# A graph network's node stages with two buffers instead of one, and its first table split inside the first gather pass

## The chip, the core and the metric

The kernel runs on one core of a Trainium2 chip. The metric is the device time of one execution in microseconds (us); here it is the median of three runs. Five engines work beside each other, each with its own queue: TensorE (PE) multiplies and transposes into PSUM, VectorE (DVE) and ScalarE (ACT) work element by element, GpSimd (POOL) does so too and issues the indirect DMAs, and SyncE (SP) issues most of the other DMAs. They meet only at semaphores.

## What is computed

Two layers of a graph network over 12500 nodes of 64 values and 412500 edges, sorted by their end node. The first is a hyperbolic attention layer, the second a message-passing layer with batch norms over edges and over nodes. Cut to what matters:

```python
h = jnp.maximum(_layernorm(x), 0.0)
# layer 0, over nodes
h = mobius_matvec(weight, h, C)                 # h @ weight.T, rescaled by row
# over edges: row = src, col = dst
dist = sqdist(h[edge[0]], h[edge[1]], C)
edge_e = jnp.exp(-leaky_relu(logmap0(C / (C + dist), C)[0], ALPHA))
h_prime = segment_sum(edge_e[:, None] * logmap0(h, C)[edge[1]], edge[0])
out = jax.nn.elu(h_prime / segment_sum(edge_e, edge[0])[:, None])
x = x + proj(expmap0(out, C), C)
h = jnp.maximum(_layernorm(x), 0.0)
# layer 1, over edges
e = _bn_relu(concat([h[src], h[dst], edge_attr]) @ Wm1 + bm1, gm1, betm1)
msg = _bn_relu(e @ Wm2 + bm2, gm2, betm2)
aggr = segment_sum(msg, src)
# over nodes; _bn_relu(x, gamma, beta) = relu(gamma * (x - mean) / sqrt(var + EPS) + beta)
u = _bn_relu(concat([h, aggr]) @ Wu1 + bu1, gu1, betu1)
x = x + _bn_relu(u @ Wu2 + bu2, gu2, betu2)
```

## The kernel before

The program is written engine by engine, in blocks (`nc.Block()`). Inside one, every engine runs its own list, and `end_phase` puts two barriers of all engines between stages. All order is written by hand: `wait_ge`, `hold` (a wait in a loop) and `consume` (a wait that takes its count back) are the waits, `chain` makes a queue wait for each of its own instructions.

Nodes stand as 98 chunks (NCH) of 128 partitions with D = 64 values each, and one chunk of padding (NC = 99). Node stages go over them in NIT = 7 rounds of CPI = 14 chunks, so one part is 128 x 896 numbers, or 128 x 1792 where rows are 128 wide. Edges stand in NBLK = 214 blocks of 16 tiles (TB) of 128 slots.

The stages in their order, with those that the change touches named in bold:

- **First node stage** (block at L249): layer norm, then seven rounds for the product with the weight. In each, VectorE copies the part to `stage` (L278), TensorE turns it by seven transposes into PSUM (L347), ScalarE copies that to `hT` (L326), TensorE multiplies (L351), VectorE copies the product out (L280). `stage`, `hT` and each PSUM area are single. Then row functions, and the table `h0_d` is stored.
- Sort of the edges into blocks (L462 on), 3000 us long.
- **First table** (block at L957), a stage of its own: SP loads the rows of `h0_d` into R0 (L960), and VectorE's `piece3` splits them into three bf16 numbers each, in T0 (L839 to L843, once for 6336 and once for 99 columns).
- **First gather pass** (block at L1045). GpSimd gathers the far node's row for each edge, 16 indirect DMAs a block (L1084), into four buffers G; TensorE picks the near node's row out of T0 with one-hots (L1126), in quarters of a block, into two PSUM areas; VectorE sums their three pieces (L1145) and multiplies with the gathered rows (L1151 to L1156). SP loads the records (L1049, L1064) and spreads slot numbers over the partitions for VectorE's one-hots (L1056, L1060, L1135). After three parts of the blocks and at the end VectorE computes distances (`part_weights`).
- Weights and first sums over edges (L1187 to L1363).
- **Middle stage** (block at L1372): division, elu, the second layer norm.
- **Second table** (block at L1428): the product of h with both halves of Wm1, seven rounds as in the first stage. VectorE copies one half out over a scratch tile into `b` (L1452, L1453), adds the bias to the other (L1454) and splits it by `piece3` into T1. When all is done SP stores `b` (L1438).
- Second gather pass, then two passes over edges with the batch norms of the messages.
- **Last stages** (blocks at L2037, L2090, L2117). The first adds the two halves of the sums (L2051), and in seven rounds VectorE puts h and the sums side by side in `stage` (L2054, L2056), TensorE turns (L2069), ScalarE copies (L2082), TensorE multiplies with Wu1 (L2074), ScalarE copies out with the bias (L2084). Then `node_stats` takes 25 lots of 500 nodes (L2026). The second does relu (L2094), product (L2106), copy out (L2096), and `node_stats` again. The third does relu (L2121), turns back (L2129), adds to X (L2138), and SP stores the whole result (L2145, L2146).

## Time and profile before

| what | value |
|---|---|
| median of 3 runs | 17072.78 us |
| lowest and highest | 17068.78 and 17084.48 us |
| the profiled execution's own time | 17093.01 us |
| its span in the trace | 17091.3 us |
| busy in the span: PE, DVE, ACT, POOL | 37%, 51%, 24%, 56% |

One execution was profiled; its rows carry every duration below, in us from the span's start. A row of the timeline has start, duration, engine and line, the tiles written and read, how many instructions were merged, and in brackets how long the engine stood idle before, and what released it. `SPq` is the issue of a DMA by SP; the DMA itself ends later, which shows in who waits for it. "remote" and "issue" are waits that the trace puts down to no instruction.

### The profile page before, as it was taken

How to read it: one execution, taken by the hardware profiler on the slowest of the kernel's cores; microseconds unless marked ns; L12 is line 12 of the kernel's file. 1: busy time of each engine (PE TensorE's matmuls, PEld its weight loads, DVE VectorE, ACT ScalarE, POOL GpSimd, SP SyncE). 2: the span in 40 equal slices, each digit the busy share in tenths (PEclk: the TensorE clock that was granted, in tenths of full speed). 3: DMA queues.
4: the chain of work that ended last, by engine and by line, in shares of the span. 5: the costliest groups of instructions: out<-in, count | busy, mean ns of one | idle time of the engine just before them, and what ended most of it. 6: DMA issues, size and time to landing. Idle time of an engine off the chain costs nothing. (4 is left out here: it accounts for less than half of the span.)

```text
span 17091.3 us, 195568 instructions
## 1 busy us (share of the span) xinstructions
PE 6354.3 (37%) x50077; PEld 5035.1 (29%) x50078; DVE 8652.0 (51%) x18303; ACT 4054.6 (24%) x7861; POOL 9635.6 (56%) x9968
## 2 busy tenths in 40 slices
PE   2444444311111111111159522323223223258996
PEld 2444444300000000000058511111111111125995
DVE  5888888623333333333268733333333333346884
ACT  1666666400000000000058400000000000024333
POOL 0555555466656665666657356666666666622773
PEclk7777777655555555555579756655655656579998
DMA  2000000133323332323444222222222222275331
GB/s 58 8 8 8 8 8 8 27 75 75 75 66 73 75 74 68 74 69 74 67 106 151 67 66 66 68 63 68 67 65 68 65 66 68 65 145 187 106 107 54
DMA packets 1142331, 1160.59 MB, mean 68 GB/s; under 512 B 688769, under 2 KB 832769, under 8 KB 1142018
## 3 DMA queue, kind: packets, MB, share of 16 engines
q1 hardware_dynamic: 845634, 680.39, 13.9%
q0 software_dynamic: 235008, 248.13, 8.6%
q10 hardware_dynamic: 61632, 231.44, 3.4%
q8 instruction: 20, 0.33, 0.0%
q14 instruction: 37, 0.30, 0.0%
HBM read 872.56 MB, written 286.75 MB: 68 GB/s over the span
## 5 line engine op out<-in xcount | busy, mean ns | idle before, releaser
L1559 POOL DMA_INDIRECT big<-b_d,big x3424 | 3284.0, 959 | 2270.7 <-POOLq L144 1232.2
L1084 POOL DMA_INDIRECT big<-h_d,big x3424 | 3273.9, 956 | 2001.9 <-issue 1189.0
L1145 DVE TENSOR_REDUCE ps<-ps 128x260 f32<-128x780 f32 x856 | 837.8, 979 | 3275.1 <-remote 1441.1
L1126 PE MATMUL ps<-big 128*128 x3424 | 737.9, 373 | 4609.0 <-issue 3388.5
L1686 DVE TENSOR_REDUCE ps<-ps 128x256 f32<-128x768 f32 x856 | 827.6, 967 | 2582.9 <-DVEq L144 1605.9
L1126 PEld LDWEIGHTS ps<-big 128*128 128x128 bf16 x3424 | 442.4, 162 | 4904.3 <-issue 4901.1
L1638 PE MATMUL ps<-big 128*128 x3424 | 608.7, 335 | 2615.9 <-issue 2130.1
L1885 POOL TENSOR_SCALAR big<-iota_f,big 128x128 f32<-128x128 f32 x1498 | 880.4, 608 | 827.7 <-DMA big<-rec_d 528.3
L1638 PEld LDWEIGHTS ps<-big 128*128 128x128 bf16 x3424 | 444.6, 160 | 2973.7 <-issue 2973.7
L777 ACT ACTIVATE big<-big 128x512 bf16<-128x512 bf16 x1736 | 1076.7, 708 | 907.1 <-ACTq L144 907.1
L1092 ACT ACTIVATE big<-big 128x16 int32<-128x16 f32 x214 | 49.1, 229 | 4899.9 <-issue 2304.5
L1620 PE MATMUL ps<-big 128*128 128x512 f32 x856 | 768.6, 1052 | 1134.6 <-PEq L144 1107.3
L1573 ACT ACTIVATE big<-ps 128x128 f32<-128x128 f32 x214 | 59.4, 278 | 4695.8 <-ACTq L144 4142.0
L747 PE MATMUL ps<-big 128*128 128x120 bf16 x12896 | 1001.4, 251 | 63.2 <-issue 59.3
L747 PEld LDWEIGHTS ps<-big 128*128 128x128 bf16 x12896 | 951.3, 118 | 87.9 <-issue 85.9
L825 POOL DMA_INDIRECT rec_d<-big x496 | 791.8, 1596 | 290.2 <-POOLq L144 160.6
L783 ACT ACTIVATE big<-big 128x512 bf16<-128x512 bf16 x1736 | 913.6, 614 | 0.0
L1283 POOL TENSOR_SCALAR big<-iota_f,big 128x128 f32<-128x128 f32 x856 | 691.1, 820 | 326.3 <-DMA big<-rec_d 288.5
L1358 PE MATMUL ps<-big 128*128 128x128 f32 x6848 | 815.8, 277 | 103.5 <-DVE big L1283 89.5
L810 POOL TENSOR_TENSOR big<-HA,big 128x624 bf16<-128x624 bf16 x124 | 153.3, 1236 | 1224.4 <-POOLq L144 1224.4
L1358 PEld LDWEIGHTS ps<-big 128*128 128x128 f32 x6848 | 782.8, 192 | 136.3 <-issue 134.0
L1961 PE MATMUL ps<-big 128*128 128x64 f32 x6848 | 789.1, 274 | 1.8 <-DVE big L1885 1.7
(409 smaller groups left out, 14488.7 us busy)
## 6 DMA issues: line engine op xcount, KB each, us to landing
big<-e_d SPq DMA_DIRECT2D x428, 512.0 KB, 3.1
rows_d<-big ACTq DMA_DIRECT2D x214, 544.0 KB
big<-rows_d SPq DMA_DIRECT2D x214, 544.0 KB, 3.2
HA<-slots_d SPq DMA_DIRECT2D x214, 512.0 KB
big<-slots_d SPq DMA_DIRECT2D x214, 512.0 KB
e_d<-big ACTq DMA_DIRECT2D x214, 512.0 KB
big<-rec_d SPq DMA_DIRECT2D x860, 64.0 KB, 2.9
big<-h_d,big POOLq DMA_INDIRECT x3424
```

The source lines that it names most:

```text
L747: m = t.matmul(o, DH[b][:, j * WS + w * P:j * WS + (w + 1) * P], EX[b][:, j * CH * L:(j + 1) * CH * L], start=False, stop=(j == J - 1))
L777: a.activation(DH[b][:, j * WS:(j + 1) * WS], iota_w, ACT.Square, scale=-1.0, bias=seg_f[b][:, j:j + 1]).then_inc(s_sq, 1)
L783: last = a.activation(o, o, ACT.Relu, scale=-1.0, bias=1.0)
L825: gp.indirect_dma_start(rec_d, bass.IndirectOffsetOnAxis(ix[b][:, w:w + 1], 0), stage[b][:, w * L * REC:(w + 1) * L * REC], None).then_inc ...
L1084: gp.indirect_dma_start(G[g][:, t * ROW:(t + 1) * ROW], None, h0_d, bass.IndirectOffsetOnAxis(idx[g % 2][:, t:t + 1], 0)).then_inc(gath[g] ...
L1126: m = t.matmul(XS[q % 2][:, n, 0:3 * D + 3], OT3[g % 2][:, o, :], T0[:, ds(chunks[o // 2] * TW, 3 * D + 3)], start=True, stop=True)
L1145: v.tensor_reduce(xrow[:, q * QT:(q + 1) * QT, :], XS[q % 2][:, :, 0:3 * D + 3].rearrange("p t (q w) -> p t w q", q=3), AX, ALU.add).then_ ...
L1358: m = t.matmul(ps[:, o:o + P], O4[g][:, n * P:(n + 1) * P], G0[g][:, n * ROW:n * ROW + P], start=(n % 2 == 0), stop=(n % 2 == 1))
L1559: gp.indirect_dma_start(G[g][:, t * D:(t + 1) * D], None, b_d, bass.IndirectOffsetOnAxis(idx[g % 2][:, t:t + 1], 0)).then_inc(gath[g], 16)
L1638: m = t.matmul(XST[q % 2][:, n // 2, n % 2, :], OT3[g % 2][:, o, :], T1[:, ds(chunks[o // 2] * (3 * D), 3 * D)], start=True, stop=True)
L1686: v.tensor_reduce(x, XSQ[q % 2], AX, ALU.add).then_inc(s_e, 1)
L1885: last = eng.tensor_scalar(u1.O[b][:, n * P:(n + 1) * P], iota_f[:, :], u1.rec[b][:, n * REC:n * REC + 1], None, ALU.is_equal)
```

## The change

- The first node stage and the second table have no `stage` any more: TensorE turns the parts where they stand in HB. `hT` is double, and so are the PSUM areas of the transposes and, in the first stage, of the products. The loops are written out, and TensorE turns part i+1 before it multiplies part i.
- In the second table ScalarE copies the `b` half from PSUM to its place, and VectorE keeps the addition and the split. A product waits for both to have left the single PSUM area. SP stores b part by part.
- The first table's own stage is gone. Its load and its split stand at the head of the first gather pass; TensorE's steps wait for the split. The scratch tiles now lie where the pass writes later (`R0t` over XY, `q2t` over W3, R0 over the edges' numbers).
- In the middle stage min(exp(U), 1) - 1 takes the place of exp(min(U, 0)) and the later - 1.
- In the last stages `stage` and `uT` are double, the sums' halves are added in each round, the statistics of the part just finished are taken in each round, the second and third stage alternate between PSUM halves, and X is stored part by part.

The core of the diff; the first stage's loop reads as the second table's with its own names, and the last stages' ScalarE, TensorE parts likewise:

```diff
-        stage = take(CPI * D)
-        hT = take(CPI * D)
+        hT = [take(W) for _ in range(2)]
+        TRO, MMO = (0, 1024), (2048, 3072)
...
-        with nc.Block() as block:
-            @block.sync
-            def _(sp):
-                sp.dma_start(R0, h0_d.rearrange("(c p) w -> p c w", p=P)).then_inc(s_in, 16)
-                sp.wait_ge(s_in, 16)
-
-            @block.vector
-            def _(v):
-                link, k = chain(v, s_v)
-                v.wait_ge(s_in, 16)
-                piece3(v, link, R0[:, :, 0:D], R0t, T0q)
-                piece3(v, link, R0[:, :, SQ:SQ + 1], q2t, T2q)
-
-        end_phase()
...
                 for g in range(4):
                     sp.dma_start(rec3[g], rec_tile[g]).then_inc(rec_in[g], 16)
+                sp.dma_start(R0, h0_d.rearrange("(c p) w -> p c w", p=P)).then_inc(s_table, 16)
...
+                t.wait_ge(t0_rdy, 1)
                 each_block(t, step)
...
+                split, _count = chain(v, s_split)
+                v.wait_ge(s_table, 16)
+                piece3(v, split, R0[:, :, 0:D], R0t, T0q)
+                piece3(v, split, R0[:, :, SQ:SQ + 1], q2t, T2q)
+                v.sem_inc(t0_rdy, 1)
...
-                link(v.tensor_scalar(V, U, 0.0, None, ALU.min))
                 v.wait_ge(s_a, 1)
+                link(v.tensor_scalar(V, V, 1.0, -1.0, ALU.min, ALU.add))
                 link(v.scalar_tensor_tensor(out=U, in0=U, scalar=0.0, in1=V, op0=ALU.max, op1=ALU.add))
-                link(v.tensor_scalar(U, U, -1.0, None, ALU.add))
...
-                with v.Fori(0, NIT) as i:
-                    v.tensor_copy(stage, HB[:, ds(i * W, W)]).then_inc(g_in, 1)
-                    hold(v, "v", g_mm, i + 1)
-                    link, done = chain(v, g_sp, loop=True)
-                    link(v.tensor_copy(SB3, PAB[:, :, D:2 * D]))
-                    link(v.tensor_copy(AG[:, ds(i * W, W)], SB))
+                for i in range(NIT):
+                    v.wait_ge(g_mm, i + 1)
                     link(v.tensor_tensor(SA3, PAB[:, :, 0:D], bm1b.unsqueeze(1).to_broadcast([P, CPI, D]), ALU.add))
+                    v.sem_inc(g_a, 1)
...
+                keep(0)
+                for i in range(NIT):
+                    if i + 1 < NIT:
+                        keep(i + 1)
+                    a.wait_ge(g_a, i + 1)
+                    a.activation(AG[:, i * W:(i + 1) * W].rearrange("p (c d) -> p c d", d=D), PAB[:, :, D:2 * D], ACT.Copy
+                                 ).then_inc(g_b, 1)
...
+                def product(i):
+                    t.wait_ge(g_cp, i + 1)
+                    if i >= 1:
+                        t.wait_ge(g_a, i)
+                        t.wait_ge(g_b, i)
...
-                v.tensor_tensor(AG[:, 0:NC * D], AG[:, 0:NC * D], u1.AG2, ALU.add).then_inc(s_w, 1)
+                def concat(i):
+                    if i >= 2:
+                        v.wait_ge(f_tr, i - 1)
+                    c = slice(i * WD, (i + 1) * WD)
+                    v.tensor_copy(stage3[i % 2][:, :, 0:D], HB[:, c].rearrange("p (c d) -> p c d", d=D)).then_inc(f_in, 1)
+                    v.tensor_tensor(stage3[i % 2][:, :, D:P], AG[:, c].rearrange("p (c d) -> p c d", d=D),
+                                    u1.AG2[:, c].rearrange("p (c d) -> p c d", d=D), ALU.add).then_inc(f_in, 1)
+                concat(0)
+                concat(1)
                 link, k = chain(v, s_v)
-                node_stats(v, link, Y1, mv1, colp[:, 2:3], colp[:, 4:5], sc1, sh1, s_a, 1)
+                for i in range(NIT):
+                    if i + 2 < NIT:
+                        concat(i + 2)
+                    v.wait_ge(f_y, i + 1)
+                    chunk_stats(v, link, Y1, i)
+                node_stats(v, link, mv1, colp[:, 2:3], colp[:, 4:5], sc1, sh1, s_a, 1)
...
+                for i in range(NIT):
+                    sp.wait_ge(f_add, i + 1)
+                    c0, c1 = i * CPI, min((i + 1) * CPI, NCH - 1)
+                    sp.dma_start(out[c0 * P:c1 * P, :].rearrange("(c p) d -> p c d", p=P), X[:, c0:c1, :]).then_inc(s_out, 16)
```

The order of the instructions, at three queues. First SP, from the end of the sort into the first gather pass; `h_d` is the table of rows, `rec_d` the records. Before:

```order
L462 UNCONDITIONAL_BRANCH
L958 UNCONDITIONAL_BRANCH
L960 DMA big<-h_d 128x99x68
L957 UNCONDITIONAL_BRANCH
L1046 UNCONDITIONAL_BRANCH
L1049 DMA big<-rec_d 128x16x8 x4
```

And after:

```order
L477 UNCONDITIONAL_BRANCH
L1047 UNCONDITIONAL_BRANCH
L1050 DMA big<-rec_d 128x16x8 x4
L1051 DMA big<-h_d 128x99x68
L1014 UNCONDITIONAL_BRANCH
```

The records' loads now stand ahead of the rows' load, and the block between them is gone.

On VectorE at the same place, before the change, the end of the split and the pass's first one-hot:

```order
L842 TENSOR_TENSOR big<-big 128x99
L843 CAST big<-big 128x99
L957 UNCONDITIONAL_BRANCH
L1131 UNCONDITIONAL_BRANCH
L1135 TENSOR_SCALAR big<-HA,iota_p 128x2048
```

And after:

```order
L1134 UNCONDITIONAL_BRANCH
L854 CAST big<-big 128x99x64
L855 TENSOR_TENSOR HA<-big 128x6336
L856 CAST big<-HA 128x99x64
L857 TENSOR_TENSOR HA<-HA,big 128x6336
L858 CAST big<-HA 128x99x64
```

The whole split has moved behind the pass's entry; its small second half and then the one-hot follow these rows.

On TensorE in the second table, transposes are the rows with `ident`. Before, one loop body:

```order
L1469 UNCONDITIONAL_BRANCH
L1469 ISA
L1472 MATMUL ps<-ident,big 128x128 x7
L1476 MATMUL ps<-big 128x256 x7
L1469 REGISTER_ALU
L1469 COMPARE_AND_BRANCH
```

And after, the first rounds of seven:

```order
L1481 UNCONDITIONAL_BRANCH
L1490 MATMUL ps<-ident,HA 128x128 x14
L1499 MATMUL ps<-big 128x256 x7
L1490 MATMUL ps<-ident,HA 128x128 x7
L1499 MATMUL ps<-big 128x256 x7
```

Two lots of transposes stand ahead of the first product, one lot ahead of each later one, and they read HA itself.

## Rows read from the trace of the kernel before

**Rows 1.** Timeline, first stage: start us, us, engine line, idle before and releaser
```profile
151.62 1.73 PE L347 MATMUL ps<-ident,big 128*128 128x128 f32 x7 [151.62 <-DMA big<-in_L_gnn_weight_dram]
...
154.53 3.22 PE L351 MATMUL ps<-big 128*128 128x128 f32 x14 [1.19 <-ACT big L326]
...
205.79 1.09 DVE L280 COPY big<-ps 128x896 f32 x1 [6.52 <-PE ps L351]
```

**Rows 2.** Timeline, end of the sort to the first gather pass
```profile
3304.33 0.82 SPq L960 DMA_DIRECT2D big<-h_d  x1
...
3322.20 3.49 DVE L839 CAST big<-big 128x6336 bf16<-128x6336 f32 x1 [30.13 <-DMA big<-h_d]
...
3354.49 0.38 DVE L843 CAST big<-big 128x99 bf16<-128x99 f32 x1
...
3356.10 4.13 SPq L1049 DMA_DIRECT2D big<-rec_d  x4
...
3374.43 0.98 DVE L1145 TENSOR_REDUCE ps<-ps 128x260 f32<-128x780 f32 x1 [0.44 <-DVEq L144]
```

**Rows 3.** Line L1084, the gathers: ns min/median/max, first and last start
```profile
L1084 POOL DMA_INDIRECT big<-h_d,big x3424: 942/947/2268, 3360.6 to 8572.8; - x191
```

**Rows 4.** Timeline of the first gather pass, three stretches of it
```profile
3388.47 0.98 DVE L1145 TENSOR_REDUCE ps<-ps 128x260 f32<-128x780 f32 x1 [10.25 <-remote]
...
3781.66 0.95 POOL L1084 DMA_INDIRECT big<-h_d,big  x1 [12.02 <-POOLq L144]
...
3784.87 0.98 DVE L1145 TENSOR_REDUCE ps<-ps 128x260 f32<-128x780 f32 x1 [0.26 <-DVEq L144]
...
5009.85 0.75 DVE L1135 TENSOR_SCALAR big<-HA,iota_p 128x2048 bf16<-128x2048 bf16 x1 [0.26 <-DVEq L1158]
...
5010.15 1.27 POOL L1084 DMA_INDIRECT big<-h_d,big  x1 [0.30 <-issue]
```

**Rows 5.** Timeline of the middle stage
```profile
9617.20 3.43 DVE L1381 TENSOR_SCALAR big<-big 128x6272 f32<-128x6272 f32 x1
```

**Rows 6.** Timeline of the second table and of its end
```profile
9719.44 6.04 PE L1476 MATMUL ps<-big 128*128 128x256 f32 x14 [1.19 <-ACT big L1464]
...
9727.53 1.09 DVE L1454 TENSOR_TENSOR big<-ps,big 128x896 f32<-128x896 f32 x1
...
9732.56 0.63 DVE L843 CAST big<-big 128x896 f32 x1
...
9836.86 0.38 SPq L1438 DMA_DIRECT2D b_d<-HA  x1
...
9854.84 0.91 DVE L1657 MEMSET big<- 128x1024 f32 x1 [18.34 <-PEq L80]
```

**Rows 7.** Timeline, first of the three last stages
```profile
16865.10 1.24 SPq L2044 DMA_DIRECT2D big<-in_L_gnn_betu_dram  x2
...
16869.80 3.07 PE L2069 MATMUL ps<-ident,big 128*128 128x128 f32 x14 [10.99 <-DVE big L2056]
...
16890.34 3.25 PE L2074 MATMUL ps<-big 128*128 128x512 f32 x8 [2.15 <-ACT big L2082]
```

**Rows 8.** Lines L2026 (twice) and L2094: ns min/median/max, first and last start
```profile
L2026 DVE BATCH_NORM_STATS2 big<-big x25: 661/664/680, 16923.2 to 16937.2; 128x6 f32<-128x500 f32 x25
...
L2026 DVE BATCH_NORM_STATS2 big<-HA x25: 661/664/680, 17008.1 to 17022.0; 128x6 f32<-128x500 f32 x25
...
L2094 ACT ACTIVATE big<-big x7: 1867/1868/1880, 16941.4 to 16999.1; 128x1792 f32 x7
```

**Rows 9.** Timeline, third of the three last stages
```profile
17026.26 1.88 ACT L2121 ACTIVATE big<-HA,big 128x1792 f32 x1 [2.30 <-PEq L2090]
...
17075.10 13.91 SPq L2146 DMA_DIRECT2D out_dram<-X  x1
```

**Rows 10.** Stretches: us, busy by engine, PEclk (TensorE clock granted), DMA share, GB/s
```profile
16880.00:16900.00 20.00, 13.57 (x63) 8.43 (x62) 3.49 (x6) 9.89 (x6) 0.00 (x0) 1.00 0.00 0
...
17026.00:17050.00 24.00, 10.37 (x46) 9.29 (x47) 3.26 (x3) 7.52 (x4) 0.00 (x0) 0.50 0.00 0
```

More of the change, by code:

```diff
@@ L242, in build @@
         s_edges = sem("n0_edges")
-        g_in, g_tr, g_cp, g_mm, g_out = (sem(f"n0g_{k}") for k in ("in", "tr", "cp", "mm", "out"))
+        g_tr, g_cp, g_mm, g_out = (sem(f"n0g_{k}") for k in ("tr", "cp", "mm", "out"))
         NPAIR = CPI // 2
@@ L1417, in build @@
         mark1 = top[0]
-        stage = take(CPI * D)
-        hT = take(CPI * D)
+        hT = [take(CPI * D) for _ in range(2)]
+        TRO = (0, 3072)
         wab = take(4 * D)
@@ L2010, in build @@
         Y2 = HA[:, 0:NCH * P]
-        stage = take(CPI * P)
-        stage3 = stage.rearrange("p (c w) -> p c w", w=P)
-        uT = take(CPI * P)
+        stage = [take(CPI * P) for _ in range(2)]
+        stage3 = [z.rearrange("p (c w) -> p c w", w=P) for z in stage]
+        uT = [take(CPI * P) for _ in range(2)]
         wu1p, wu2p = take(P), take(P)
@@ L2022, in build, with chunk_stats, node_stats @@
         WD = CPI * D
-        def node_stats(v, link, Y, mv, gamma, beta, sc, sh, s_act, count):
-            for n in range(25):
-                last = v.bn_stats(nst[:, n * 6:(n + 1) * 6], Y[:, n * (N // 25):(n + 1) * (N // 25)])
-            link(last)
+        def chunk_stats(v, link, Y, i):
+            done = lambda n: min(n * W // NS5, 25)
+            for n in range(done(i), done(i + 1)):
+                ins = v.bn_stats(nst[:, n * 6:(n + 1) * 6], Y[:, n * NS5:(n + 1) * NS5])
+                if n == 24:
+                    link(ins)
+        def node_stats(v, link, mv, gamma, beta, sc, sh, s_act, count):
             link(v.bn_aggr(mv, nst))
@@ L2092, in _, with relu @@
             def _(a):
-                with a.Fori(0, NIT) as i:
-                    a.activation(stage, Y1[:, ds(i * W, W)], ACT.Relu, bias=sh1, scale=sc1).then_inc(f_z, 1)
-                    hold(a, "a", f_mm, i + 1)
-                    a.activation(Y2[:, ds(i * W, W)], ps[:, 0:W], ACT.Identity, bias=colp[:, 1:2]).then_inc(f_y, 1)
+                def relu(i):
+                    if i >= 2:
+                        a.wait_ge(f_mm, i - 1)
+                    a.activation(stage[i % 2], Y1[:, i * W:(i + 1) * W], ACT.Relu, bias=sh1, scale=sc1).then_inc(f_z, 1)
+                relu(0)
+                for i in range(NIT):
+                    if i + 1 < NIT:
+                        relu(i + 1)
+                    a.wait_ge(f_mm, i + 1)
+                    a.activation(Y2[:, i * W:(i + 1) * W], ps[:, i % 2 * 2048:i % 2 * 2048 + W], ACT.Identity, bias=colp[:, 1:2]
+                                 ).then_inc(f_y, 1)
                 a.wait_ge(s_v, 3)
@@ L2119, in _ @@
             def _(a):
[L2120 to L2122 removed]
+                for i in range(NIT):
+                    if i >= 2:
+                        a.wait_ge(f_tr, i - 1)
+                    a.activation(stage[i % 2], Y2[:, i * W:(i + 1) * W], ACT.Relu, bias=sh2, scale=sc2).then_inc(f_z, 1)
             @block.tensor
             def _(t):
[L2126 to L2127 removed]
+                for i in range(NIT):
+                    t.wait_ge(f_z, i + 1)
+                    if i >= 2:
+                        t.wait_ge(f_add, i - 1)
                     for c in range(CPI):
[L2129 removed]
+                        o = i % 2 * 2048 + c * P
+                        m = t.transpose(ps[:, o:o + P], stage[i % 2][:, c * P:(c + 1) * P], ident[:, :])
                     m.then_inc(f_tr, 1)
```

187 lines of the change are left out of this document (107 added, 80 removed).

## The prediction

> **What bounds the kernel now.** I read the page's slices first: for most of the span GpSimd is busy and TensorE is not, and no engine is full. Then I read the timeline of each stage that the diff touches, and asked of each what the engine that starts next was waiting for. The five node stages are chains. In the first stage's loop one buffer of each kind makes TensorE, ScalarE and VectorE take turns: from the first transposes at 151.6 to the last copy's end at 206.9 seven rounds take 55.3 us, 7.9 each, of which TensorE works 1.73 + 3.22 [rows 1]. The table stage between the sort and the first gather pass is the most visible hole: SP asks for the rows at 3304.33, they are there at 3322.20, VectorE splits them until 3354.87, and only then does the pass load its records (3356.10) and gather (3360.6) [rows 2, 3]. The second table needs 135.4 us from its first product at 9719.44 to the next stage's first instruction at 9854.84, and 18 of them follow one store that begins when all is computed [rows 6]. The last three stages compute, then take statistics over everything (25 x 0.585 = 14.6 us, twice), and store at the end (13.9 us) [rows 8, 9].
>
> The gather pass itself decides what the early start is worth, so it has to be understood. GpSimd issues 16 gathers per block, one per 0.95 + 0.30 us, so 20.0 us a block. 214 blocks take 5212 us [rows 3], 24.4 a block, so it stands 4.4 us a block, waiting for one of four buffers. VectorE's reductions come 10.25 + 0.98 = 11.2 us apart while gathers are issued, and 0.98 + 0.26 = 1.24 us apart soon after GpSimd has stood still (here after 12.0 us) [rows 4]. The two are coupled: GpSimd stands until VectorE catches up, and VectorE catches up only when it stands.
>
> **The change, part by part.** All in us of the profiled execution.
>
> *First stage's loop.* The staging copy goes, transposes read the part in place, and hT and PSUM have two buffers. TensorE runs transposes of round i+1, then the product of round i. ScalarE's copy (about half of 1.87 for twice the width [rows 8], so 0.9, an estimate) and VectorE's 1.09 hide behind it. It still starts at 151.6, for the weights' load. At half clock seven rounds cost 7 x 4.95 + some 2 = 36.6, at full clock 7 x 2.5 + 2 = 20. I take 25, since TensorE is now busy without breaks: where it was busy 13.57 of 20 us the granted clock was 1.00, where 10.37 of 24 it was 0.50, the 1.2 GHz level [rows 10]. Saved: **30**, bounds 19 and 35.
>
> *First table inside the pass.* Removed: the stage and one pair of barriers. SP now issues the four record loads first, then the rows' load; GpSimd can begin 4.5 us after 3304.3, as it now does after 3356.1 [rows 2, 3], so at 3308.8 instead of 3360.6: 51.8 earlier. The rows' load moves 4.1 back and runs beside gathers: it took 17.9, I bound it by 18 and 27, so 3326 to 3336. Behind it in SP's queue stand the first slot store and slot broadcast, which nobody needs before the split is over. The split, ten chained instructions, takes 3354.87 - 3322.20 = 32.7 and ends at 3359 to 3368; TensorE waits for it. The first reduction is then near 3367 instead of 3374.4. GpSimd has issued its four blocks by 3389 and must stand for block 0; it stands, so VectorE turns quick and frees it at about 3394, after a stand of 5. From there on I expect the pass to repeat its own pattern, earlier by nearly the whole head start. I take **50**. The upper bound is 57, if VectorE's start 7 earlier shortens the first long stand as well; the lower is 30, if block 0 is freed at the slow step of 11.2 twice more. That part is the least sure.
>
> Here a price of the split's cover has to be weighed. A VectorE one-hot of 0.75 us at 5009.85 lies over a gather that took 1.27 us instead of 0.95, so 0.3 us was lost [rows 4]. Of the split's large instructions the first cast lasts 3.49; the other four share the remaining 32.7 - 3.5 - 1.9 = 27.3, 6.8 each, so only the first is of a quick kind like the one-hot.
>
> The Trainium skill says (SBUF — State Buffer, "SBUF: two separate sides") that a VectorE copy or cast in a two-port mode holds the port pair for the whole instruction, and GpSimd cannot write the descriptors of its DMAs meanwhile. The gather beside the one-hot agrees with it. By that rule and the one quick cast the head start falls by 3.5 us; if all three held it, by 17.
>
> *Middle stage.* One pass over 6272 elements goes (ScalarE takes the exponential of U itself, and min and -1 are one instruction behind it); ScalarE's part is unchanged. Saved: **3.4** [rows 5].
>
> *Second table.* Gone per round: the staging copy, two of VectorE's copies out, the loop's branch. ScalarE makes the rows of b from PSUM. Added: a product waits for VectorE's addition and ScalarE's copy of the round before (one PSUM area). Behind that wait TensorE has only later rounds; the transposes of the next one stand ahead of it. VectorE's remaining chain lasts from 9727.53 to 9733.19, 5.7, with the handover 5.8 [rows 6]. Lead-in: the second lot of transposes stands ahead of the first product, which moves 1.7 back and ends near 9727.2. At full clock VectorE is the bound: 7 x 5.8, so 9767.8. At half clock a round is product 6.04, addition 1.09, copy 0.9 and handovers, 8.2: 9727.2 + 6 x 8.2 + 5.8 = 9782.2. The stores of earlier parts hide, since a seventh of 13.9 is 2.0; the last lands within a microsecond or two of VectorE's end. With 2.5 for store and barrier the memset now at 9854.84 comes at 9770 to 9785. Saved: 70 to 85, I take **82**, since its TensorE is busy most of a round; upper bound 88, without the 2.5.
>
> *Last three stages.* First: the addition over 6336 elements (6.75) becomes part of each round's second copy, but the transposes cannot begin earlier: the last small load is issued until 16866.34, and the record loads of the gather pass were there, and turned into indices, within 4.5 of their issue [rows 2, 3]; I take 2.9, so 16869.2 and not 16869.8. A round is transposes 1.7 (half of 3.07), product 3.25, copy out 1.75 of which part shows, because statistics (25/7 x 0.585 = 2.1) and the next concatenation (1.75) share VectorE with it: 5.2 to 5.8, against 6.9. First product done by 16881.5, six rounds of 5.6, copy, and the last four statistics 2.3: 16919.3 instead of 16937.8 [rows 7, 8]. Saved: **18.5**, bounds 14 and 22. Second: 16941.4 to 17022.7 is 81.2 [rows 8]. With two PSUM halves ScalarE is the bound at full clock, 2 x 1.87 + 0.25 = 4.0 a round: 1.9 + 3.3 + 7 x 4 + 2.3 = 35.5; at half clock TensorE is, 6.5 a round: 52. I take 36, saved **45**, bounds 29 and 49. Third: transposes of 3.07 at half clock, ScalarE's 1.9 at full: the last addition comes 19 to 25 after 17026.3, then one small store, 2.0 of movement and 2.3 to land. The end of the span at 17091.3 is 65.0 after 17026.3 [rows 9]; now it is 26 + 2.2. Saved: **37**, bounds 33 and 41.
>
> Sum: 30 + 50 + 3.4 + 82 + 18.5 + 45 + 37 = 266. The profiled execution took 17093.0, so 16827; it stood 20.2 above the median of 17072.8, so **16807** for the median. All low bounds together save 198 (16875), all high ones 295 (16778).
>
> **Rivals.**
> 1. *The clock stays at half in the node loops.* For it: in the last stage, where TensorE was busy under half the time, it shows 0.50 [rows 10]. Against: it is now busy nearly throughout. Then 19, 50, 3.4, 72, 18.5, 29 and 33 are saved, 225: 16848.
> 2. *The pass follows its consumers.* GpSimd's head start is spent standing, and only the earlier first reduction counts, 5 instead of 50: 221, so 16852. For it: GpSimd already stands 4.4 us a block. Against: the reductions speed up ninefold whenever it stands [rows 4].
> 3. *The split locks GpSimd out.* 3.5 + 6.8 + 6.8 + 1.1 = 18 of the head start is lost: 32 instead of 50, 16825.
> 4. *The pass falls into another rhythm (slower than before).* A different lead at the start could make GpSimd stand its 12.0 us after every two blocks, 6.0 a block instead of 4.4: 214 x 1.6 = 342 lost, 17149. It outweighs all the rest once a block stands 4.4 + 266/214 = 5.6 us. Against: the buffers, the code of the pass and so its repeating pattern are the same.
> 5. *The change doesn't do what it says*: unrolled loops and extra waits eat the overlap, and savings stay within 0.2%. Against: each wait that goes has its releaser in the rows, and the releaser is gone or moved.
>
> **How the numbers follow.** Forecast 0.60, rival 1 0.12, rival 2 0.15, rival 3 0.07, rival 4 0.03, rival 5 0.02, and 0.01 for what I don't see. 16775 to 16880 takes in the bounds and rivals 1 to 3. 0.2%, 34 us, is about what a measurement of this kernel can tell from no change. Faster by more: 0.95; within: 0.02; slower: 0.03.
>
> **What would show it.** Right: the first gather within 5 us of the sort's end, the split over before 3370 and the pass's last gather near 8523 (rival 2: near 8568; rival 3: gathers missing beside the casts); the clock column at 1.00 in the last stages' loops (rival 1: 0.5 to 0.6); the memset behind the second table some 53 us after its first product, not 135; statistics ending 2 to 3 us after the last copy out; the end 28 us after the last stage's first relu. Wrong: a pass longer than 24.4 us a block, or a store whose last part lands late because all parts queue.

## The result

The changed kernel takes 16772.7 us (median; 16770.2 to 16776.5) against 17070.8 (17068.2 to 17084.5) for the kernel before: ratio 0.9824, 95% interval 0.9807 to 0.9841, so 298 us less. The sign was forecast; the time is 34 us lower than the 16807 forecast and 2.3 us below the range's low end of 16775. The two profiled executions, 17093.0 and 16773.8 us, are 319 apart, because that of before was a long one of its kind.

### The profile page after: what moved, and what is told of

Its sections match the earlier page's. It is cut to its first block and busy times, and to the rows that moved or that the text cites. A ratio compares the mean times of both kernels' runs of the same rounds, so it can differ in the third digit from the quotient of the medians.

```text
span 16772.1 us, 195035 instructions
## 1 busy us (share of the span) xinstructions
PE 6291.0 (38%) x50077; PEld 4991.2 (30%) x50078; DVE 8618.8 (51%) x18273; ACT 4060.1 (24%) x7868; POOL 9626.2 (57%) x9968
```

## The profile after, beside the rows of before

Timeline of the first node stage after; columns as in [rows 1].

```profile
151.51 3.25 PE L353 MATMUL ps<-ident,HA 128*128 128x128 f32 x14 [151.51 <-DMA big<-in_L_gnn_weight_dram]
...
154.55 2.95 PE L362 MATMUL ps<-big 128*128 128x128 f32 x14
...
159.66 0.93 PE L353 MATMUL ps<-ident,HA 128*128 128x128 f32 x7
160.43 1.73 PE L362 MATMUL ps<-big 128*128 128x128 f32 x14
...
170.74 1.09 DVE L280 COPY big<-ps 128x896 f32<-128x896 f32 x1 [0.47 <-PE ps L362]
```

The start is the same, since the weights' load decides it. The first transposes and the first product run at the half-clock durations of before; from 157 on a round is 0.93 + 1.73, back to back. The last copy starts at 170.74 instead of 205.79 [rows 1]: 35.1 saved, where I took 30 and had 35 as the upper bound.

Timeline from the end of the sort to the first reduction.

```profile
3270.64 1.22 SPq L1051 DMA_DIRECT2D big<-h_d  x1
3270.85 0.99 POOL L1086 DMA_INDIRECT big<-h_d,big  x1 [10.91 <-POOLq L144]
...
3290.90 3.79 POOL L1086 DMA_INDIRECT big<-h_d,big  x1 [0.30 <-issue]
3291.14 3.49 DVE L854 CAST big<-big 128x6336 bf16<-128x6336 f32 x1 [37.07 <-DMA big<-h_d]
...
3294.67 6.76 DVE L855 TENSOR_TENSOR HA<-big 128x6336 f32<-128x6336 f32 x1
3294.99 7.25 POOL L1086 DMA_INDIRECT big<-h_d,big  x1 [0.30 <-issue]
...
3301.46 6.76 DVE L856 CAST big<-HA 128x6336 bf16<-128x6336 f32 x1
3302.55 0.94 POOL L1086 DMA_INDIRECT big<-h_d,big  x1 [0.30 <-issue]
...
3308.25 6.76 DVE L857 TENSOR_TENSOR HA<-HA,big 128x6336 f32<-128x6336 f32 x1
3308.79 7.04 POOL L1086 DMA_INDIRECT big<-h_d,big  x1 [0.30 <-issue]
```

The first gather moves from 3360.6 [rows 3] to 3270.85; less the 38.0 that all work is early by here, that is the forecast 51.8. But three gathers take 3.79, 7.25 and 7.04 us instead of 0.94. They stand beside the quick cast (3.49) and the two subtractions, whose inputs both lie in SBUF (6.76). The slow casts of 6.76 hold nothing up: the gather at 3302.55 takes 0.94. The cost is 3.79 + 7.25 + 7.04 less 3 x 0.94, so 15.3 of the head start.

The Trainium skill (SBUF — State Buffer, "SBUF: two separate sides") says that VectorE takes the port pair it shares with GpSimd for a whole instruction, also when an operation has two SBUF inputs and GpSimd's own reads SBUF. The trace agrees: the two gathers end 0.81 and 0.82 behind the ends of the subtractions. I had weighed only the half of that rule on casts and copies.

The same lines as [rows 6]: the second table and its end.

```profile
9597.56 3.25 PE L1490 MATMUL ps<-ident,HA 128*128 128x128 f32 x14 [112.26 <-DMA big<-in_L_gnn_bm_dram]
...
9600.60 3.77 PE L1499 MATMUL ps<-big 128*128 128x256 f32 x14
...
9604.49 1.09 DVE L1462 TENSOR_TENSOR big<-ps,big 128x896 f32<-128x896 f32 x1 [12.55 <-PE ps L1499]
...
9639.88 1.09 DVE L1462 TENSOR_TENSOR big<-ps,big 128x896 f32<-128x896 f32 x1 [1.87 <-PE ps L1499]
...
9647.19 0.91 DVE L1684 MEMSET big<- 128x1024 f32 x1 [1.86 <-PEq L1634]
```

Six rounds take 35.4 us, 5.9 each, as forecast (5.8). From the first product the memset comes after 46.6, not 53. The last row waits 1.86 for the stores, not 18.34.

The statistics' line, as in [rows 8]; rows of the timeline, two products and a relu of ScalarE in the second of the last stages, and the last addition of the third; and stretches as in [rows 10] (PEclk is the third figure from the end): first loop, second table, the three last stages.

```profile
L2056 DVE BATCH_NORM_STATS2 big<-big x25: 662/665/682, 16675.1 to 16708.4; 128x6 f32<-128x500 f32 x25
L2056 DVE BATCH_NORM_STATS2 big<-HA x25: 661/665/682, 16721.6 to 16744.0; 128x6 f32<-128x500 f32 x25
```

```profile
16730.26 6.69 PE L2174 MATMUL ps<-big 128*128 128x512 f32 x16 [0.20 <-ACT big L2154]
16731.75 1.87 ACT L2154 ACTIVATE big<-big 128x1792 f32<-128x1792 f32 x1
...
16765.51 1.09 DVE L2211 TENSOR_TENSOR X<-X,ps 128x896 f32<-128x896 f32 x1 [0.69 <-PE ps L2202]
```

```profile
155.20:171.90 16.70, 15.50 (x131) 15.31 (x130) 7.68 (x8) 5.10 (x6) 0.00 (x0) 1.00 0.00 1
9592.00:9600.00 8.00, 2.44 (x12) 2.44 (x13) 0.00 (x0) 0.65 (x1) 0.00 (x0) 0.50 0.08 17
9604.00:9640.00 36.00, 25.45 (x121) 20.74 (x119) 31.07 (x37) 9.54 (x11) 0.00 (x0) 0.95 0.34 77
16690.00:16708.00 18.00, 11.92 (x45) 6.23 (x42) 9.55 (x16) 9.34 (x6) 0.00 (x0) 1.00 0.00 0
16712.00:16744.00 32.00, 24.68 (x56) 10.94 (x56) 14.55 (x25) 24.34 (x14) 0.00 (x0) 0.87 0.00 0
16748.00:16772.00 24.00, 14.75 (x98) 13.57 (x98) 7.62 (x7) 12.85 (x7) 0.00 (x0) 0.78 0.60 134
```

Each loop begins at the lower level (0.50: 1.2 GHz) and is at the upper one for most of its rounds; the third of the last stages does its first three rounds of transposes in 7.76 us and then two rounds in 3.52. In the kernel before, the same five loops had 0.63, 0.59, 0.92, 0.69 and 0.54 on the mean. The statistics now lie inside the loops.

The whole difference, from the same landmarks in both traces:

| part | before | after | saved | my term (bounds) |
|---|---|---|---|---|
| first loop's last copy | 205.8 | 170.7 | 35.1 | 30 (19 to 35) |
| sort and what stands before it | 3091.2 | 3088.3 | 2.9 | none |
| first table and first pass, last scatter to last gather | 5275.8 | 5197.1 | 78.7 | 50 (30 to 57) |
| middle stage | 83.3 | 79.8 | 3.5 | 3.4 |
| second table, memset to memset | 145.6 | 55.7 | 89.9 | 82 (70 to 88) |
| second gather pass, first to last gather | 5280.6 | 5267.4 | 13.2 | none |
| other stages over edges | 2769.7 | 2786.2 | -16.5 | none |
| last stages, one by one | 76.6, 84.8, 68.5 | 54.6, 35.6, 27.3 | 22.0, 49.2, 41.2 | 18.5, 45, 37 |
| all | | | 319.2 | 266 |

The touched node stages save 240.9 where my terms add up to 215.9. The pass saves 78.7 here, and untouched stages move by 3 to 17 either way. How much of that belongs to the change, this pair of traces can't say.

## Experiments

Medians in us, ratios to the kernel before on the same chip. The chips differ: the kernel before takes 16979 to 17071 on them, so only ratios and differences on one chip are compared. Three more runs (before_b, before_c, n0_unrolled_b) are single executions.

| run | median | before | ratio (95%) |
|---|---|---|---|
| rep_before | 16981.6 | 16988.9 | 0.9996 (0.9987 to 1.0006) |
| rep_after | 16699.7 | 16988.9 | 0.9832 (0.9815 to 0.9848) |
| e_pass | 16952.0 | 16988.9 | 0.9980 (0.9970 to 0.9989) |
| hold_split | 16713.2 | 16988.9 | 0.9842 (0.9825 to 0.9858) |
| e_nopass | 16735.9 | 16992.0 | 0.9851 (0.9834 to 0.9867) |
| free_split | 16682.8 | 16992.0 | 0.9815 (0.9799 to 0.9832) |
| weights_first | 16634.9 | 16992.0 | 0.9790 (0.9774 to 0.9807) |
| warm | 16624.3 | 16992.0 | 0.9785 (0.9768 to 0.9801) |
| nopass_b | 16743.2 | 16978.7 | 0.9860 (0.9845 to 0.9875) |
| hold_b | 16710.5 | 16978.7 | 0.9847 (0.9834 to 0.9861) |
| after_b | 16697.5 | 16978.7 | 0.9837 (0.9823 to 0.9850) |
| best | 16615.7 | 16978.7 | 0.9790 (0.9776 to 0.9803) |
| e_n0 | 17006.5 | 17052.3 | 0.9973 (0.9962 to 0.9984) |
| n0_unrolled | 17068.4 | 17052.3 | 1.0011 (1.0002 to 1.0021) |
| ends | 16800.1 | 17052.3 | 0.9854 (0.9837 to 0.9870) |

**Both kernels again** (no edit).

> The kernel before, once more, for a second trace of it. In the first trace the 214 blocks take 5212.1 us from the first to the last gather, in the changed kernel 5185.2: 26.9 less, beside the 51.8 of the earlier start. Theory A: the 26.9 are no work of the change but the spread between two executions (the profiled one of before lay 20.2 above its median); then this trace has 5185 to 5200 and an own time near 17071. Theory B: the changed start makes every block a little shorter; then this trace has 5208 to 5216 again and the times differ elsewhere.

> The changed kernel, once more. Ratio 0.9824 to 0.9826 to the kernel before. Theory A: its pass is anywhere from 5180 to 5200 us, the two ranges of before and after overlap. Theory B: within 4 of 5185.2. The node stages repeat to 1 us: first stage's loop ends near 171.8, the memset behind the second table 53 to 56 us after the first vector instruction of its stage.

The gathers' line of three executions of the kernel before and two of the changed one (rep_before, before_b, before_c; rep_after, after_b), as in [rows 3]:

```profile
L1084 POOL DMA_INDIRECT big<-h_d,big x3424: 938/944/2318, 3359.6 to 8513.6; - x191
```

```profile
L1084 POOL DMA_INDIRECT big<-h_d,big x3424: 938/944/2299, 3359.3 to 8543.1; - x191
```

```profile
L1084 POOL DMA_INDIRECT big<-h_d,big x3424: 939/947/2284, 3361.1 to 8530.7; - x191
```

```profile
L1086 POOL DMA_INDIRECT big<-h_d,big x3424: 941/947/7026, 3268.0 to 8414.7; - x191
```

```profile
L1086 POOL DMA_INDIRECT big<-h_d,big x3424: 938/944/7248, 3265.6 to 8433.4; - x191
```

With the old pass it takes 5154.0, 5183.8 and 5169.6 (5212.1 in the first trace), with the new one 5146.7 and 5167.8 (5185.2). The ranges overlap, so the 26.9 are no steady gain of the change and theory B falls; but the spread is wider than the 5180 to 5200 that I gave theory A. The node stages repeat to 2 us, and the second table's saving is 87.8 to 90.

> The kernel before again, for one more trace of the old pass: 5140 to 5215 from first to last gather, whatever the chip. If 5200 and more never comes again, the first trace of before was a rare one, and the 76 us that the first pair of traces showed for the table inside the pass are for a good part that draw.

> The kernel before beside it on the same chip: that stage again 1716 to 1734, the sort stage 3028 to 3030, the pass anywhere from 5150 to 5215.

Both came out as expected. The 5212 did not come again in eight more traces of kernels with the old pass (5122.9 to 5183.8).

**The pass alone and the nodes alone.** e_pass takes from the diff only its four places in the first table and the first gather pass; e_nopass and nopass_b take all but those.

> The kernel before with one part of the change alone: the first table is split inside the first gather pass. My forecast for this part was 50 us, less the some 15 that the trace shows as lost to gathers that stand beside the split's large instructions: 35 to 42, ratio 0.9975 to 0.9980. Theory A: about 40 to 55 in medians, ratio 0.9968 to 0.9977, pass 5185 to 5200 in its trace. Theory B: 77 in medians, ratio 0.9955. Rival 2 (the pass follows its consumers): 5 to 8, ratio 0.9996.

> The changed kernel with the first table's own stage put back: node stages only. By the two traces so far the node stages save 35.1 + 3.5 + 88 to 90 + 22 to 24 + 49.3 + 41.3 = 239 to 243, where my sum had 216. Theory S (the node terms were each sized too small): ratio 0.9855 to 0.9862, 240 to 246 us. Theory P (the node stages save what I forecast, and the pass the rest): 216, ratio 0.9873. It has the pass of before, so its length is one more sample of that: if the 26.9 us were spread between executions, it lies anywhere from 5150 to 5215.

> The node stages alone once more, now on the same chip as the next three, in five rounds: what the table inside the pass is worth is this kernel less the changed one. On two different chips it was 289 - 256 = 33. My forecast was 50, with the split's lock 32 to 35. Expected 30 to 40 (theory L: the head start counts, less what the gathers lose beside the split); 5 to 8 by rival 2; 50 or more if the head start counts in full in spite of the lock.

e_pass saves 36.9, which fits the forecast less the lock, and neither 77 nor 8. The nodes alone save 256.1 and 235.5, around the 240 to 246 of theory S, not the 216 of theory P. What the pass adds to them is 16743.2 - 16697.5 = 45.7 on one chip, and 289.2 - 256.1 = 33 across two. So it is worth 33 to 46 in three comparisons, each uncertain by some 20. These medians hold more than the pass. From the last scatter to the last gather the traces of nopass_b and after_b differ by 28.7, and the second pass and the stretch behind it, which nobody touched, by another 17.7; e_pass is 54.9 ahead of rep_before at its last gather and loses 17 of that in stages behind it.

**GpSimd held until the split is over** (hold_split, hold_b).

```diff
                     gp.sem_inc(stored[g], 16)
+                gp.wait_ge(t0_rdy, 1)
```

> The changed kernel in which GpSimd waits for the end of the split before its first gather, so the first gather moves from 3270.9 to about 3324 and no gather stands beside the split any more; TensorE and VectorE begin as early as they did. If the pass follows GpSimd's head start: 53 later less the 15.5 that the gathers lost beside the split, 35 to 40 slower than the changed kernel. If it follows its consumers (rival 2): 0 to 5 slower. In between if the head start is spent in part: 10 to 30.

> The changed kernel with GpSimd waiting for the end of the split, once more beside the others. Its first gather stands where that of the kernel without the change in the pass stands (63.7 us after the sort's last scatter), and the traces of the two reach the last gather after the same 5122.9. So by theory L it is as fast as the one with the table's own stage, within 8, and 25 to 36 slower than the changed kernel. If it is the removed stage itself that counts and not GpSimd's start (rival 2): within 8 of the changed kernel.

Timeline rows of hold_b: the first gather and the first reduction.

```profile
3318.11 0.99 POOL L1087 DMA_INDIRECT big<-h_d,big  x1 [63.10 <-POOLq L144]
...
3325.79 0.98 DVE L1155 TENSOR_REDUCE ps<-ps 128x260 f32<-128x780 f32 x1 [0.44 <-issue]
```

GpSimd starts some 52 later, 37 after the lock is taken off, and the kernel is 13.5 and 13.0 slower than the changed one on the same chip. The traces show 28.1 and 23.7 from the last scatter to the last gather. So my reading, that the head start counts nearly in full, falls: between a third and three quarters of it arrives, 10 to 30, the middle case of what I wrote for hold_split. The expectation for hold_b, as fast as the kernel without the pass, missed too: it is 33 faster. Some 20 of that stand in untouched stages (second pass 5243.0 and 5246.3 against 5255.1 and 5254.0; the stretch from its last gather to the last stages 1724.3 and 1724.1 against 1734.9 and 1734.5). The first reduction comes 7.7 us after the first gather instead of 13.8 [rows 2, 3], because the one-hots are ready, but at the last gather the traces show 5.0 of that in hold_b and nothing in hold_split (5186.7 against 5186.5). That is what rival 2 had as its whole gain.

The traces also show where a part of the head start goes. Counted from the last scatter, the 65th block begins at 1516.6 in after_b and at 1548.6 in hold_b, so 32 of the 37 are still there. Then GpSimd stands while VectorE computes the distances of the first part of the blocks. Rows of after_b, then of hold_b: VectorE's first large step of that, and the first gather behind the stand.

```profile
4835.02 1.54 DVE L1027 TENSOR_TENSOR HA<-HA,big 128x1024 f32<-128x1024 f32 x1
...
4876.03 0.94 POOL L1086 DMA_INDIRECT big<-h_d,big  x1 [63.45 <-POOLq L144]
```

```profile
4855.53 1.53 DVE L1027 TENSOR_TENSOR HA<-HA,big 128x1024 f32<-128x1024 f32 x1
...
4896.53 0.94 POOL L1087 DMA_INDIRECT big<-h_d,big  x1 [41.56 <-POOLq L144]
```

VectorE is only 20 earlier there, counted from the last scatter. GpSimd stands 63.45 instead of 41.56 (and, before the block ahead, 2.7 instead of 12.9), and behind it the lead is 20. hold_split and rep_after show the same step, from 31 to 19. The pass has three such stands. From the first gather of the block ahead to the first one behind, they take 61.1 to 84.9, 67.9 to 84.8 and 60.1 to 76.4 us in the twenty traces, so much of the spread between executions arises there.

**The split without the lock** (free_split).

```diff
+                a.wait_ge(s_table, 16)
+                for part, (c0, c1) in enumerate(HALF):
+                    if part >= 2:
+                        a.wait_ge(s_split, 5 * (part - 1))
+                    a.activation(R0p[part], R0[:, c0:c1, 0:D], ACT.Copy).then_inc(s_ps, 1)
...
-                piece3(v, split, R0[:, :, 0:D], R0t, T0q)
+                for part, (c0, c1) in enumerate(HALF):
+                    v.wait_ge(s_ps, part + 1)
+                    piece3(v, split, R0p[part], R0p[part], T0q[:, c0:c1])
```

HALF are four parts of at most 25 chunks, R0p their places in PSUM.

> The changed kernel in which ScalarE first copies the rows to PSUM in four parts and VectorE splits from there, so that none of its large instructions has both inputs in SBUF or is a cast from SBUF. If it is those that hold the gathers up: all gathers beside the split take 0.95 to 1.3 us, and the fourth block's first gather comes at 72 us after the sort's last scatter instead of 87.5. If the rows' load holds them up (rival): 7 us gathers remain. The split ends 3 to 8 later. In time: 15 of head start less 5 for the split; if a head start counts, 5 to 12 faster than the changed kernel, else 0 to 5 slower; about 0.9825 to 0.9835.

Rows of free_split's timeline, and the gathers' line:

```profile
3289.27 1.83 DVE L855 TENSOR_TENSOR ps<-ps,big 128x1600 f32<-128x1600 f32 x1
3289.49 0.94 POOL L1091 DMA_INDIRECT big<-h_d,big  x1 [0.30 <-issue]
```

```profile
L1091 POOL DMA_INDIRECT big<-h_d,big x3424: 938/944/1623, 3265.7 to 8408.8; - x191
```

The longest gather of the pass is 1.62 us, that beside a subtraction out of PSUM 0.94. The fourth block begins 75.5 after the last scatter instead of 87.5, and not 15 earlier, because ScalarE makes the third block's indices behind its copies and GpSimd waits 3.3 for them. The lock is shown, and its cause: with one input in PSUM it is gone, and the rows' load, which runs as before, holds nothing up. The subtractions also write to PSUM here; that this is not what frees the gathers is shown by the pass's multiplications, which read PSUM and SBUF and write SBUF: in the changed kernel 41 gathers lie beside one of them and nothing else, and each takes 0.94 or 0.95. In time the two kernels can't be told apart (0.9815 and 0.9832, intervals overlap); its lead over rep_after, counted from the last scatter, is 17 us at block 60, 35 at block 80, 13 at block 130 and 4 at the last, with a jump at each of the three stands.

**Weights ahead of the edges** (weights_first), and TensorE kept at work (warm, on top of it).

```diff
                 sp.wait_ge(s_w, 1)
                 for h in range(2):
                     sp.dma_start(wblk[h * D:(h + 1) * D, h * D:(h + 1) * D], w0t).then_inc(s_st, 16)
+                for t_, a_ in ((s_i, src), (d_i, dst)):
...
+                t.wait_ge(s_v, 12)
+                for _n in range(60):
+                    t.transpose(ps[:, 0:P], ident[:, :], ident[:, :])
                 t.wait_ge(s_st, 32)
```

> The changed kernel with the two loads of the first stage's weights put ahead of the edges' loads in SP's queue. TensorE now waits for them until 151.5, while the rows that it turns are ready at 73.7 and VectorE is free for the copies at 87.4. The loop then ends near 104 instead of 171.8, all later work 65 to 70 earlier, and ratio 0.978 to 0.980. If the edges' loads land so much later that the next stage waits for them: less than 40.

> The one with the weights first, in which TensorE does transposes that nobody reads in five gaps just before a node stage (60, 24, 28, 9 and 9 of them). My node terms were too small chiefly for products that I costed at half clock. If the clock rises after a few us of unbroken work, as the rows of the changed kernel suggest (first round's product 2.95 us, the next ones 1.73), then with that work done ahead the first rounds run at full clock: first stage's first product at 1.73, second table's first product near 3.3 instead of 3.77, last stage's first transposes 1.7 instead of 3: some 2 us a stage, 5 to 8 in all. If the first rounds are slow for another reason, nothing changes, or it is 1 to 3 slower for transposes that overrun.

Timeline of weights_first, then of warm, at the first round of the first stage and (warm, last row) of the second table.

```profile
73.73 3.22 PE L353 MATMUL ps<-ident,HA 128*128 128x128 f32 x14 [73.73 <-DVE HA L213]
...
76.75 2.62 PE L362 MATMUL ps<-big 128*128 128x128 f32 x14
...
100.72 1.09 DVE L280 COPY big<-ps 128x896 f32<-128x896 f32 x1 [0.47 <-PE ps L362]
```

```profile
73.72 1.72 PE L356 MATMUL ps<-ident,HA 128*128 128x128 f32 x14 [1.33 <-DVE HA L213]
...
75.68 1.83 PE L365 MATMUL ps<-big 128*128 128x128 f32 x14 [0.24 <-ACT big L328]
...
9467.92 3.29 PE L1504 MATMUL ps<-big 128*128 128x256 f32 x14 [0.24 <-ACT big L1475]
```

The weights bring 70 in the loop's end, as expected, and some 68 in medians (357 less than the kernel before, where the changed kernel has 289 on another chip). In warm the first transposes fall from 3.22 to 1.72 and the first products from 2.62 to 1.83 and from 3.77 to 3.29. So a loop's slow first round is the clock alone, and work just ahead lifts it. It is worth 2.8 in all in the trace, less than the 5 to 8 expected, since VectorE or a load is late in the same places. The medians are 10.6 apart and their intervals overlap.

**Written out, but with one buffer** (n0_unrolled, twice), and the new loop alone (e_n0: the diff's four places in the first stage).

```diff
-                with v.Fori(0, NIT) as i:
-                    v.tensor_copy(stage, HB[:, ds(i * (CPI * D), CPI * D)]).then_inc(g_in, 1)
-                    hold(v, "v", g_mm, i + 1)
+                for i in range(NIT):
+                    v.tensor_copy(stage, HB[:, i * (CPI * D):(i + 1) * (CPI * D)]).then_inc(g_in, 1)
+                    v.wait_ge(g_mm, i + 1)
```

> The kernel before with the new loop of the first stage alone. The loop saves 35 us, as in all traces of the changed kernel. Open is the sort stage behind it, which nobody touched: from the first stage's end to the last scatter it takes 3029.1 to 3029.9 in three traces with the old loop and 3022.4 to 3027.0 in ten with the new one. If that comes with the new loop: 3022 to 3026 here, and 38 to 42 saved in all (ratio 0.9975 to 0.9978). If it comes with another part: 3029 to 3030.

> The kernel before with the first stage's loop written out seven times instead of branching, everything else as it was: one buffer, the staging copy, the same waits. A round's work in a row is 0.63 + 1.73 + 0.92 + 3.22 + 1.09 = 7.6 of 7.9 us, so the buffers must bring the 35 us: the loop's end moves by 1 to 3 us only. If it was branches and register waits, 10 or more. For the sort stage: if its 5 us hang on where the later instructions lie in memory, this one shows some change too (not 3029.1 to 3029.9); if on the two buffers' loop itself, 3029.5.

> The kernel before with the first stage's loop written out, once more for its trace. In its first one the loop saved 4 and the sort 7, yet its median was 19 above that of before; the stage before the last three took 1750.8 where the kernel before had 1716.3, 1721.6 and 1733.6. If the place of the code decides it: 1745 to 1755 again, and the sort stage 3021 to 3023. If it was one execution's spread: anywhere from 1716 to 1735.

e_n0 saves 45.8, where 38 to 42 were expected: 36.6 in the loop, the rest mostly in the sort. Written out alone, the loop's last copy starts at 201.5: 4 of the 35 are branches and register waits (1 to 3 were expected), 31 the buffers and the clock. A stretch of n0_unrolled shows a mean of 0.83 where TensorE stands a third of the time, and one round of it shows what that is made of, transposes at one level and a product at the other:

```profile
160.00:180.00 20.00, 13.21 (x62) 11.55 (x61) 3.56 (x5) 2.75 (x3) 0.00 (x0) 0.83 0.00 1
```

```profile
174.42 0.98 PE L347 MATMUL ps<-ident,big 128*128 128x128 f32 x7 [1.72 <-DVE big L278]
...
176.41 3.25 PE L351 MATMUL ps<-big 128*128 128x128 f32 x14 [1.01 <-ACT big L326]
```

The sort answers too, with a surprise. Its scatters, in before_b and in n0_unrolled_b, and behind them the products of the second batch norm stage, in before_c and in n0_unrolled_b:

```profile
L825 POOL DMA_INDIRECT rec_d<-big x496: 954/958/3894, 456.2 to 3295.4; - x166
```

```profile
L825 POOL DMA_INDIRECT rec_d<-big x496: 954/958/3597, 451.0 to 3283.6; - x166
...
L1826 PE MATMUL ps<-big,w2blk x856: 592/592/1193, 15141.9 to 15580.0; 128*128 128x512 f32 x172
```

```profile
L1826 PE MATMUL ps<-big,w2blk x856: 592/592/1193, 15146.0 to 15559.7; 128*128 128x512 f32 x172
```

From its first to its last scatter the sort takes 2839.1 to 2841.0 in all five traces with the old first stage and 2832.1 to 2834.7 in all fifteen in which it is written out, with one buffer or two. The products of a stage that nobody touched take 438.1 from the first to the last, where before_c has 413.7: so in both traces of n0_unrolled (438.2 and 438.1) and in no other kernel (413.4 to 415.9). These 24 us outweigh the 4 of its loop and the 7 of its sort, and its median is 16 above that of before. Code moved the times of stages that it does not belong to, reproducibly. That it is the place of the instructions in memory is my guess; nothing here changes the place alone.

**Store and statistics back at the end** (ends).

```diff
-                for i in range(NIT):
-                    sp.wait_ge(g_b, i + 1)
...
+                sp.wait_ge(g_b, NIT)
...
-                    v.wait_ge(f_y, i + 1)
+                    v.wait_ge(f_y, NIT)
```

> The changed kernel with three things put back: the rows of b are stored in one piece when all are made, and both statistics of the last stages are taken when all products are copied out. By the rows of before: the store and its landing show with 10 to 14 us in the second table's stage (64.9 us from its first memset to the next pass's first gather becomes 75 to 79); each lot of statistics shows with 25 x 0.585 less the last four = 12.3 (54.6 becomes 67, 35.6 becomes 48). In all 35 to 39 slower than the changed kernel, ratio near 0.986.

Timeline of ends: the next stage's first memset, behind the store of b.

```profile
9661.62 0.91 DVE L1681 MEMSET big<- 128x1024 f32 x1 [14.66 <-PEq L1631]
```

The table's stage is 12.4 longer than after (77.4 against 64.9), the statistics cost 11.1 and 12.8: 36.3 in all, each within 1.2 us of what the rows of before gave. These terms were sized right.

**All at once** (best: weights_first, warm and free_split).

> All at once: weights ahead of the edges' loads (65 by the last comparison), the transposes that nobody reads ahead of the node stages (2.9 by the trace), and the split by way of PSUM (12 to 15 of head start). 75 to 85 faster than the changed kernel, ratio 0.978. If the split by way of PSUM is worth nothing in the end (its lead had shrunk from 15 to 4 at the last block of its first trace): 65 to 72, ratio 0.9786.

It takes 16615.7, 81.8 less than the changed kernel beside it, ratio 0.9790 to the kernel before (after_b: 0.9837): faster than both, nearly all of it by the weights' order, for weights_first alone has 0.9790 and warm 0.9785.

## Why the prediction was wrong, and where it was right

- **Start and split of the first pass: right; its end: not.** On the forecast's scale, which leaves out the 38.0 by which all is early there, the first gather stands at 3308.9 (forecast 3308.8), the split's end at 3361.9 (3359 to 3368), the first reduction at 3365.6 (3367), but the last gather at 8494.1 (8523).
- **The step that failed: the node loops were costed with slow TensorE rounds that do not occur, and one of them with too long a round of ScalarE.** Six terms of 215.9 measure 240.9, each at or over its upper bound but that of the middle stage, and this put the time below the range. The 25 by part:
  - First loop, 5.1: I took 25 between 20 at the upper clock and 36.6 at the lower. From the first transposes to the last copy's end it takes 20.3.
  - Second table, 7.9: I let the first product end 17.9 behind the stage's first memset, as if it took 6.04 as in [rows 6]. It took 3.77 and began 2.8 earlier, because staging copy and handover were gone, so the first addition came 13.0 after that memset, where it was 18.3. Another 2.5 is my 82 instead of the 84.5 that my own sum gives at full clock.
  - First of the last stages, 3.5: the transposes begin 6.8 after the stage's first instruction instead of 7.9, and a round takes 5.35 instead of 5.6.
  - Second, 4.2, and this one is no matter of the clock. I had it at the upper clock, but took ScalarE's round for 2 x 1.87 + 0.25 = 4.0. Its copy out takes 1.75, and a round takes 3.44 (two of them from 16730.26 to 16737.15).
  - Third, 4.2: I had half-clock transposes in the range, and 26 to the small store's end. Only three rounds are slow; the last addition starts 17.4 after the first relu and ends at 18.5, where I gave 19 to 25.

  I had bounded the loops by a clock that stays low, and in the first loop, the table and the third stage took a value inside, though my own argument (TensorE is busy without breaks) named the upper end.
- **The first table inside the pass: sized 50, measured 33 to 46 (e_pass 36.9).** The forecast's first half holds: the head start of 51.8 is there. The lock, which I left out of the sum but for a rival, takes 15.3 of it. And what is left does not count in full: 13 in medians, 24 to 28 in traces, for GpSimd's part. The step "the pass repeats its pattern, earlier by nearly the whole head start" was wrong in size. The 78.7 of the first pair hold a long execution of before: its 5275.8 from the last scatter to the last gather are 28 to 58 above the three other traces of that kernel.
- **Rivals.** 1 (clock stays half): no, 0.78 to 1.00. 2 (pass follows its consumers): no, but in part; the earlier first reduction gives 0 to 5, and at the first stand the lead of GpSimd shrinks to that of VectorE. 3 (split locks GpSimd out): real, at 15.3 instead of 18, by the cast and the two subtractions and not by all casts; I gave it 0.07, and a share of my forecast's 0.60 belonged there. 4 (another rhythm, slower) and 5: no, since no trace of the changed kernel has a longer pass than the first one of before, and the loops overlap as written.
- **What was in no term:** 4 to 9 us of the sort that come with written-out code, and shifts of 10 us in other stages.
- The sum: 241 of nodes, some 7 of the sort, 33 to 46 of the pass are 281 to 294, beside 298 measured on the first chip and 281 to 289 on the others. Two errors, 25 too little and some 10 too much, offset each other in part: that the time came within 34 of the forecast is partly luck.

What stays open: why a head start of 37, of which 20 are left behind the first stand, arrives as 13 in medians and 24 to 28 in traces, what decides how long a stand is, and what in the moved code changes the sort and the second batch norm stage.

## What to carry to other kernels

When a chain is turned into a pipeline that keeps TensorE busy, cost its rounds at the upper clock and only the first ones at the lower (one to three of seven here); a bound for "the clock stays low" belongs in the range, not in the value. Before work is laid beside gathers that GpSimd issues, look at each VectorE instruction there: here a quick cast and operations with two SBUF inputs stopped them for their whole length, and a copy in PSUM avoided it. And a trace of before is one draw: of a gather pass of 5200 us it can be 40 us from the middle, and kernels with written-out code had untouched stages moved by 7 and 24 us, so a term of 50 is only tested by single-part kernels on one chip.

## What was not expected of the hardware

- A gather issued by GpSimd took 7.25 and 7.04 us beside subtractions of 6.76 with two SBUF inputs, 3.79 beside a quick cast of 3.49, and 0.94 or 0.95 beside casts of 6.76, beside the split out of PSUM and beside multiplications with one input in PSUM.
- A small store that SP issued 1.8 us after the rows' load held SP's queue for 15.71 us, where the next two took 3.36 and 2.96:

```profile
3272.43 15.71 SPq L1058 DMA_DIRECT2D slots_d<-big  x1
```

- In each of the changed kernel's five loops the granted clock was 0.50 when TensorE began and 1.00 after its first one to three rounds; in the second table it fell back once, and a product took 4.95 instead of 3.26. In a loop in which TensorE stood a third of the time it was 0.83 on the mean, with transposes of 0.98 and products of 3.25.
- The same program differs by up to 90 us between chips (16979 to 17071), while ratios agree to 0.0013.
